# Second attention of a two-layer kernel: query and key rows turned once and stacked through DRAM, output parts summed before a projection over 256 rows

## The chip, the cores and the metric

The kernel runs on one core of one Trainium2 chip. The metric is the device time of one execution in microseconds (us). Three runs of the kernel before gave a median of 1408.72 us, from 1408.67 to 1409.96.

## The reference, cut to what matters

The whole program is two layers over 8 batches of 256 tokens with 256 channels. Each layer norms its input, runs an attention and a feed-forward network on it, and adds attention times silu(feed-forward) to the input. Only the second layer's attention is touched:

```
qkv = einsum('bld,ed->ble', x, w_qkv)            # x: (8, 256, 256)
q, k, v = split into 3 x 16 heads of 16 channels
q = q * rsqrt(mean(q*q) + 1e-6) * q_norm_w       # over the 16 channels
k = k * rsqrt(mean(k*k) + 1e-6) * k_norm_w
scores = einsum('bhqd,bhkd->bhqk', q, k) * 16 ** -0.5
attn = softmax(scores)
out = einsum('bhqk,bhkd->bhqd', attn, v) -> (8, 256, 256)
s = einsum('bld,ed->ble', out, w_proj) + b_proj
g = silu(shared experts + 8 routed experts, top 2)
x = x + s * g
```

Products keep float32 accuracy by splitting each operand into a high part (rounded) and a low part (the rest), and by summing high x high, high x low and low x high: three matmuls for one product (the helper `product`, lines 58 to 60).

## The kernel before, in words

`stage_layer1` is the last of three stages. Its work is laid out in slots, numbered n from -16 to 132; the slots 0 to 127 each carry one head of one batch (n = 16 b + u, head u of batch b). In a slot TensorE runs, in this order: the scores of head n+1 (L1820, two matmuls), the slot's job items, the turn of head n-1's probabilities (L1830, four transposes), and the product of head n-2's probabilities with the values (L1844, four matmuls).

The job items are everything else: T (turn the normed input), Q0 and Q1 (queries and keys), V (values), P0 and P1 (projection of the batch before), L and C (router), g, G, u, U, D0, D1 (the 56 tiles of the feed-forward network, half a product each), and S0 to S7. A planner assigns them to slots: every kind has a cost in units, in which three matmuls of 512 columns are 6 and four transposes 4; the attention's jobs stand at fixed slots; the network's pieces fill each slot up to SLOT_GOAL, less UNIT for the fixed part (30.6 and 10), and from slot -12 to -1 up to EARLY_GOAL (14). Added up over slots 0 to 127 this gives 20.7 units of items per slot, and 202 units before slot 0.

Each engine walks the slots in order and executes its own list for each. VectorE, per slot: the row maximum of head n+1 (L1680), the low part of turned head n-2 (L1684), batch work by u (sum of squares L1602 at u = 2, scaling of the rows L1612 at u = 6, router steps), the first half of the slot's items, the reciprocal of head n+1's sums (L1714), the second half of the items. ScalarE: the high part of the turned head n-2 (L1473), the exponentials of head n+1 (L1465), items. GpSimd: batch work (Newton steps at u = 3, 4, 5, `weigh` L1312 at u = 7, spreading the values), the normalisation of head n+1 (L1337), the network's low parts and masks.

A job writes one of three PSUM banks in turn and waits until the job three before it has given its bank back. There is one bank of scores: the scores of head n wait for the exponentials of head n-1. Turn n-1 and values n-2 in slot n both wait for the low part of head n-2 (L1684).

How queries and keys reach the scores: for every head each row is laid out four times beside itself as high and low parts (`k_hi` L1449 and `q_hi` L1457 on ScalarE, `k_lo` L1619 on VectorE, `q_lo` L1317 on GpSimd). For every pair of heads an S job transposes four 128 x 128 blocks of these (L1773), and ScalarE copies the result out of PSUM to `zq` and `sk` (L1420, L1421), which hold three pairs.

How the output leaves: four heads share one accumulation in PSUM of 128 rows, 16 rows of each head's product with the high part of the values and 16 of that with the low part. It is split as it is (`out_hi` L1479, `out_lo` L1655, at u = 2, 6, 10, 14) and the projection runs over four such groups, 512 rows: 12 matmuls for each P job.

SyncE issues all loads: for each network tile its weights (`load_gu` L1242, `load_d` L1247), masks (`load_cb` L1262), each after a wait for the buffer to come free.

## Time and profile before

| | |
|---|---|
| median of three runs | 1408.72 us |
| the profiled execution itself | 1408.91 us |
| span of its records | 1407.1 us |
| PE (TensorE matmul) busy | 1368.9 us, 97% |
| DVE (VectorE) busy | 920.9 us, 65% |
| ACT (ScalarE) busy | 820.0 us, 58% |
| POOL (GpSimd) busy | 761.9 us, 54% |
| granted TensorE clock, mean | 0.998 |
| DMA engines, mean rate | 118 GB/s |

Busy is the time in which an engine had a recorded instruction running. PE's matmuls overlap at their ends, so what one costs is the distance from its start to the next start, not its length. Idle time of an engine that is not the bound costs nothing.

### The profile page before, as it was taken

Reading aid. Unit: us, or ns where it says so; the run is one execution under the profiler, and the core shown is the slowest. Engines: PE = TensorE matmul, PEld = TensorE weight load, DVE = VectorE, ACT = ScalarE, POOL = GpSimd, SP = SyncE. Lnnn points to the kernel's source line nnn. Section 1 sums busy time; section 2 is a strip of 40 time slices with the busy share of each in tenths; the row PEclk is TensorE's granted clock in tenths of the full one; section 3 lists DMA queues with packets and bytes.
Section 4 is the critical chain, followed back from the end, with each engine's and each line's share of the span. In section 5 each row is a group of like instructions: output and inputs, shape, how many; then the busy total and the mean of one; then the engine's idle time right before and its main releaser. Section 6 shows DMA issues by size and latency. Waiting matters only on the chain. (4 is left out here: it accounts for less than half of the span.)

```text
span 1407.1 us, 25856 instructions
## 1 busy us (share of the span) xinstructions
PE 1368.9 (97%) x8950; PEld 1221.1 (87%) x8950; DVE 920.9 (65%) x1793; ACT 820.0 (58%) x2172; POOL 761.9 (54%) x757
## 2 busy tenths in 40 slices
PE   9999899999999999999999999899999999999997
PEld 7887798999899989998999888788889888889887
DVE  6655566565656565656665665677777878777764
ACT  5553444554544555445544544378787788778873
POOL 2651433454434454435544443477669677777764
PEclk9999999999999999999999999999999999999999
DMA  5995333334332343223433334144233242342442
GB/s 197 323 330 198 85 91 89 92 80 120 100 94 52 101 130 99 75 75 98 114 86 94 113 75 165 68 122 150 83 98 123 68 150 84 120 120 92 143 122 90
DMA packets 85681, 165.64 MB, mean 118 GB/s; under 512 B 16720, under 2 KB 27664, under 8 KB 83248
## 3 DMA queue, kind: packets, MB, share of 16 engines
q1 hardware_dynamic: 85552, 163.99, 38.3%
q8 instruction: 73, 1.20, 0.4%
q14 instruction: 56, 0.46, 0.1%
HBM read 99.90 MB, written 22.09 MB: 87 GB/s over the span
## 5 line engine op out<-in xcount | busy, mean ns | idle before, releaser
L775 POOL TENSOR_TENSOR a_pr<-a_pr,a_ri 128x512 f32<-128x512 f32 x128 | 133.5, 1043 | 299.1 <-DVE a_ri L955 299.1
L832 ACT ACTIVATE a_pr<-a_score,a_nb 128x256 f32<-128x256 f32 x256 | 119.3, 471 | 266.3 <-DVE a_nb L947 266.3
L1337 POOL TENSOR_TENSOR l_pr<-l_pr,l_ri 128x512 f32<-128x512 f32 x128 | 133.5, 1043 | 119.0 <-DVE l_ri L1714 118.1
L1465 ACT ACTIVATE l_pr<-l_score,l_nb 128x256 f32<-128x256 f32 x256 | 119.2, 472 | 80.8 <-DVE l_nb L1680 80.2
L58 PE MATMUL a_job<-s_xs,s_wh 128*128 128x512 f32 x384 | 153.9, 401 | 1.0 <-PEq L221 1.0
L60 PE MATMUL a_job<-s_xs,s_wl 128*128 128x512 f32 x384 | 151.7, 395 | 0.0
L59 PE MATMUL a_job<-s_xs,s_wh 128*128 128x512 f32 x384 | 151.3, 394 | 0.0
L947 DVE TENSOR_REDUCE a_nb<-a_score 128x2 f32<-128x512 f32 x128 | 88.5, 692 | 85.0 <-PE a_score L1026 83.3
L1680 DVE TENSOR_REDUCE l_nb<-l_score 128x2 f32<-128x512 f32 x128 | 87.5, 684 | 34.0 <-PE l_score L1820 33.4
L960 DVE TENSOR_TENSOR a_pt<-a_turn,a_pt 128x512 fp32r<-128x512 f32 x128 | 87.5, 683 | 24.2 <-ACT a_pt L840 24.2
L1844 PE MATMUL l_out<-s_wh,l_vp 128*128 128x256 f32 x512 | 91.6, 300 | 0.9 <-DVE s_wh L1684 0.9
L58 PE MATMUL l_job<-l_xs,s_wl 128*128 128x512 f32 x224 | 90.6, 405 | 1.7 <-DVE l_ga L1594 1.7
L1684 DVE TENSOR_TENSOR s_wh<-l_turn,s_wh 128x512 fp32r<-128x512 f32 x128 | 87.2, 681 | 5.5 <-ACT s_wh L1473 5.4
L1473 ACT ACTIVATE s_wh<-l_turn 128x512 fp32r<-128x512 f32 x128 | 76.5, 597 | 23.4 <-PE l_turn L1830 23.0
L60 PE MATMUL l_job<-l_xs,s_wl 128*128 128x512 f32 x224 | 88.9, 397 | 0.0
L59 PE MATMUL l_job<-l_xs,s_wl 128*128 128x512 f32 x224 | 88.6, 396 | 0.0
L955 DVE RECIPROCAL a_ri<-a_sm 128x2 f32<-128x2 f32 x128 | 21.2, 166 | 102.3 <-ACT a_pr L832 102.3
L1830 PE MATMUL l_turn<-s_ident,l_pr 128*128 128x128 f32 x512 | 77.9, 275 | 10.5 <-DVE s_wh L1684 9.4
L60 PEld LDWEIGHTS a_job<-s_xs,s_wl 128*128 128x128 f32 x384 | 72.1, 188 | 16.9
L1830 PEld LDWEIGHTS l_turn<-s_ident,l_pr 128*128 128x128 f32 x512 | 59.3, 140 | 28.6 <-issue 13.6
L844 ACT ACTIVATE a_ot<-a_out 128x512 fp32r<-128x512 f32 x64 | 38.8, 606 | 77.8 <-PE a_out L60 76.8
L58 PEld LDWEIGHTS a_job<-s_xs,s_wh 128*128 128x128 f32 x384 | 72.2, 188 | 11.3 <-issue 1.4
(257 smaller groups left out, 4780.3 us busy)
## 6 DMA issues: line engine op xcount, KB each, us to landing
s_wl<-wgu_scratch SPq DMA_DIRECT2D x56, 512.0 KB, 4.8
a_sk<-a_rotk SPq DMA_DIRECT2D x384, 64.0 KB, 2.0
a_sq<-a_rotq SPq DMA_DIRECT2D x256, 64.0 KB, 2.0
s_xs<-xn_scratch SPq DMA_DIRECT2D x14, 1024.0 KB, 5.6
l_wd<-wd_scratch SPq DMA_DIRECT2D x56, 256.0 KB, 2.7
a_raw<-in_w SPq DMA_DIRECT2D x30, 256.0 KB, 3.0
wgu_scratch<-f_split SPq DMA_DIRECT2D x14, 512.0 KB, 4.7
f_praw<-in_moe_w SPq DMA_DIRECT2D x14, 384.0 KB, 4.5
```

The costliest lines, as they stand in the source:

```text
L58: pe.matmul(out, lh, rh, start=first, stop=False)
L59: pe.matmul(out, lh, rl, start=False, stop=False)
L60: return pe.matmul(out, ll, rh, start=False, stop=last)
L775: pool.tensor_tensor(e, e, ri[:, n % 2, :].unsqueeze(2).broadcast_to([P, 2, SEQ]), ALU.mult)\
L832: i = act.activation(pr[:, n % 2, t, :], PS[n % 2][:, t * SEQ:(t + 1) * SEQ], ACT.Exp, bias=nb[:, n % 2, t:t + 1], accum_out=sm[:, n % 2, ...
L947: dve.tensor_reduce(nb[:, (n + 1) % 2, :], PS[(n + 1) % 2][:, :].rearrange("p (t k) -> p t k", t=2), AX.X, ALU.max, negate=True).then_inc( ...
L960: dve.tensor_tensor(pt[:, n % 2, 1, :], PT[:, :], pt[:, n % 2, 0, :], ALU.subtract).then_inc(S["turn_free"], 1)
L1337: pool.tensor_tensor(e, e, ri[:, n % 3, :].unsqueeze(2).broadcast_to([P, 2, SEQ]), ALU.mult)\
L1465: i = act.activation(pr[:, n % 3, t, :], PS[n % NPS][:, t * SEQ:(t + 1) * SEQ], ACT.Exp, bias=nb[:, n % 3, t:t + 1], accum_out=sm[:, n % 3 ...
L1680: dve.tensor_reduce(nb[:, (n + 1) % 3, :], PS[(n + 1) % NPS][:, :].rearrange("p (t k) -> p t k", t=2), AX.X, ALU.max, negate=True).then_in ...
L1830: i = pe.transpose(PT[:, kc * SEQ + t * P:kc * SEQ + (t + 1) * P], pr[:, n % 3, t, kc * P:(kc + 1) * P], ident[:, :])
L1844: i = pe.matmul(PO[:, 0:SEQ], vp[:, kc, a, e * P:(e + 1) * P], pt[:, n % 2, q, kc * SEQ:(kc + 1) * SEQ], start=(e == 0 and kc == 0 and q = ...
```

## The change

1. Queries and keys of a head quartet are interleaved by a host-side reordering of the weight's columns (`head_columns`), so that a plain 128-column block of the scaled rows holds eight heads. One job X0 and one X1 for each batch (at u = 8 and 10, for the first batch 8 and 9) transpose these blocks; ScalarE writes the high and VectorE the low part into `tqk`.
2. SyncE stores `tqk` to DRAM (`store_stack`, four DMAs for each X job) and loads it back in stacked form, each high and low row repeated, for four heads at a time (`load_stack`, three DMAs every four slots, first due three slots before the scores that read them). The S jobs, `k_hi`, `q_hi`, `k_lo`, `q_lo` and the copies to `zq` and `sk` are gone.
3. SyncE's list is woven by slots: before each wait of `load_gu`, `load_d` and `store_combine` it issues the stack transfers due up to the slot in which that wait ends (`stack_until`).
4. The high and low product rows of an output group lie 64 rows apart. ScalarE copies 64 rows (`out_low`), VectorE adds the other 64 (`out_sum`), two groups fill 128 rows, and only then are these split (`out_hi` on ScalarE after the exponentials, `out_lo` on VectorE after the reciprocal, every eighth slot, at u = 2 and 10). A P job reads two groups instead of four: 6 matmuls. The first stage splits one piece of projection weights less.
5. The planner's numbers: P costs 6, X costs 4, SLOT_GOAL is 28.1, EARLY_GOAL 18. The same sum over the slots now gives 18.2 units of items per slot for slots 0 to 127, and 250 before slot 0.
6. The sum of squares and the scaling read the rows with a stride of four elements.

```
-    UNIT, SLOT_GOAL, EARLY_GOAL = 10, 30.6, 14
+    UNIT, SLOT_GOAL, EARLY_GOAL = 10, 28.1, 18
...
-        m, r = divmod(n + 4, H1)
-        if r % 2 == 0 and 0 <= m < BATCH:
-            jobs.append((f"S{r // 2}", m))
+        if b + 1 < BATCH and u in X_AT(b + 1):
+            jobs.append((f"X{X_AT(b + 1).index(u)}", b + 1))
...
+                def store_stack(m, half):
+                    wait_free(sp, (f"X{half}", m))
+                    for low in range(2):
+                        sp.dma_start(qs_dram[m % 2, half, :, :, low]..., tqk[:, half, 0, low, :]...)
+                        sp.dma_start(ks_dram[m % 2, half, :, low]..., tqk[:, half, 1, low, :]...)
+                def load_stack(i):
+                    pair = i * PER_LOAD
+                    ...
+                    if p % 4 == 0:
+                        sp.wait_ge(tqk_out[p // 4], 16 * 4 * (m + 1))
+                    if pair >= NSTK:
+                        sp.wait_ge(S["score_full"], 2 * (pair + PER_LOAD - NSTK))
+                    for h in range(2):
+                        sp.dma_start(zq[64 * h:64 * h + 64, h, at, :]..., ...)
+                    sp.dma_start(sk[:, at, :]..., ...)
+                def transfers(n):
+                    m, u = n // H1 + 1, n % H1
+                    if m < BATCH and u - 1 in X_AT(m):
+                        store_stack(m, X_AT(m).index(u - 1))
+                    if n % (2 * PER_LOAD) == 0 and 0 <= n // (2 * PER_LOAD) + 1 < N // (2 * PER_LOAD):
+                        load_stack(n // (2 * PER_LOAD) + 1)
...
+                    elif name[0] == "X":      # ScalarE, then VectorE
+                        act.activation(tqk[:, half, :, 0, :], bank[:, :]..., ACT.Copy)
+                        dve.tensor_tensor(tqk[:, half, :, 1, :], bank[:, :]..., tqk[:, half, :, 0, :], ALU.subtract)
...
-                    for a in range(VG):       # P job
+                    for a in range(VB):
                             i = product(pe, bank[:, 0:D], [ot[:, q, a, ...] ...], [wp[:, q, a, :] ...], ...)
...
+                    if u % (2 * PER_LOAD) == 0:      # scores
+                        pe.wait_ge(zq_in[stack_of(i)], ...)
+                        pe.wait_ge(sk_in[stack_of(i)], ...)
...
-                    own(dve.tensor_reduce(ss[:, :], sqr[:, :, :].rearrange("p t (g d) -> p (t g) d", d=D1), AX.X, ALU.add))
+                    own(dve.tensor_reduce(ss[:, :]..., sqr[:, :, :].rearrange("p t (g d q) -> p (t g) q d", d=D1, q=4), AX.X, ALU.add))
```

## Rows read from the trace of the kernel before

**Rows 1.** Windows of stage three: busy us of each engine, clock, DMA.

```profile
889.90:918.70 28.80, 25.95 (x134) 20.86 (x135) 20.32 (x50) 13.48 (x30) 17.46 (x25) 0.94 0.27 92
918.70:1383.90 465.20, 451.61 (x3153) 406.40 (x3152) 351.68 (x746) 360.57 (x1057) 342.14 (x419) 1.00 0.38 115
```

**Rows 2.** Tile view of the scores: count, min/median/max ns, first and last start.

```profile
L1820 PE MATMUL l_score<-l_sk,l_zq x256: 275/280/386, 918.7 to 1383.9; 128*128 128x256 f32 x128
```

**Rows 3.** Waits between 920 and 1385 us: total, times, longest.

```profile
PE l_turn L1830 <- DVE s_wh L1684: 9.4, 14, 1.3
```

**Rows 4.** Timeline of PE: start us, length us; slots 50 to 52.

```profile
1105.37 0.41 PE L1820 MATMUL l_score<-l_sk,l_zq 128*128 128x256 f32 x2
1105.61 0.38 PE L1773 MATMUL l_job<-s_ident,l_stq 128*128 128x128 f32 x2
...
1105.96 0.48 PE L58 MATMUL l_job<-l_xs,s_wl 128*128 128x512 f32 x1
...
1107.43 0.60 PE L1830 MATMUL l_turn<-s_ident,l_pr 128*128 128x128 f32 x4
1107.79 0.72 PE L1844 MATMUL l_out<-s_wh,l_vp 128*128 128x256 f32 x4
1108.35 0.40 PE L1820 MATMUL l_score<-l_sk,l_zq 128*128 128x256 f32 x2
...
1112.85 0.28 PE L58 MATMUL l_job<-s_wl,l_ot 128*128 128x256 f32 x1
...
1114.27 0.38 PE L1773 MATMUL l_job<-s_ident,l_stq 128*128 128x128 f32 x2
```

**Rows 5.** Groups by line and shape, 900 to 1400 us: busy, mean ns, idle before.

```profile
L1465 ACT ACTIVATE l_pr<-l_score,l_nb 128x256 f32<-128x256 f32 x256 | 119.2, 472 | 80.8 <-DVE l_nb L1680 80.2
...
L1684 DVE TENSOR_TENSOR s_wh<-l_turn,s_wh 128x512 fp32r<-128x512 f32 x128 | 87.2, 681 | 5.5 <-ACT s_wh L1473 5.4
...
L1420 ACT ACTIVATE l_zq<-l_job 64x256 fp32r<-64x256 f32 x128 | 48.0, 375 | 1.5 <-PE l_job L1773 0.5
...
L1619 DVE TENSOR_TENSOR l_stk<-l_qk,l_stk 128x256 fp32r<-128x256 f32 x32 | 23.1, 762 | 0.0
```

**Rows 6.** Timeline of PE, the start of slot 34 (batch 2, u = 2).

```profile
1047.71 0.39 PE L1820 MATMUL l_score<-l_sk,l_zq 128*128 128x256 f32 x2
```

**Rows 7.** Timeline of DVE in slot 34.

```profile
1049.35 0.41 DVE L1655 TENSOR_TENSOR l_ot<-l_out,l_ot 128x256 fp32r<-128x256 f32 x1
1049.68 1.21 DVE L1602 TENSOR_REDUCE l_ss<-l_sqr 128x64 f32<-128x1024 f32 x1
...
1051.26 0.16 DVE L1714 RECIPROCAL l_ri<-l_sm 128x2 f32<-128x2 f32 x1
1051.34 0.67 DVE L1598 TENSOR_TENSOR l_ga<-l_ga,l_job 128x512 f32<-128x512 f32 x1
```

**Rows 8.** Timeline of POOL, the weighing of batch 3's queries.

```profile
1067.91 1.30 POOL L1312 TENSOR_TENSOR l_qk<-l_qk,s_nqk 128x512 f32<-128x512 f32 x1
```

**Rows 9.** Timeline of PE, the start of slot 40 (batch 2, u = 8).

```profile
1069.00 0.28 PE L1820 MATMUL l_score<-l_sk,l_zq 128*128 128x256 f32 x1
```

**Rows 10.** Tile view of wgu_scratch: SyncE's issue, ns; then issue to landing.

```profile
L1242 SPq DMA_DIRECT2D s_wl<-wgu_scratch x54: 319/427/586, 890.3 to 1373.2; - x54
...
DMA to landing us min/median/max: 3.3/4.7/10.7
```

**Rows 11.** Page, part 6: DMA issues of stage two, KB each, us to landing.

```profile
a_sk<-a_rotk SPq DMA_DIRECT2D x384, 64.0 KB, 2.0
```

**Rows 12.** Timeline at the head and the tail of stage three.

```profile
909.40 0.51 PE L58 MATMUL l_job<-l_xs,s_wl 128*128 128x512 f32 x1 [1.67 <-DVE l_ga L1594]
...
1398.36 0.42 DVE L1655 TENSOR_TENSOR l_ot<-l_out,l_ot 128x256 fp32r<-128x256 f32 x1 [1.25 <-ACT l_ot L1479]
1398.70 1.28 DVE L1668 SCALAR_TENSOR_TENSOR l_y<-l_yt,l_y 128x512 f32<-128x512 f32 x2
...
1399.57 0.28 PE L58 MATMUL l_job<-s_wl,l_ot 128*128 128x256 f32 x1
```

More of the change, by code:

```diff
@@ L40 @@
 TB = SEQ // P
-VG, VSTRIDE, VBLK = 4, 160, 640
+VG, VB, VSTRIDE, VBLK = 4, 2, 144, 576
+VHALF = VG * D1
 ROOT_BITS = float(0x5F3759DF - (1 << 22))
@@ L1196, in stage_layer1 @@
         gu_in = l1.gu_in
+        zq_in, sk_in = ([n_.sem(f"{s}_in{i}") for i in range(NSTK // PER_LOAD)] for s in ("zq", "sk"))
+        tqk_out = [n_.sem(f"tqk_out{i}") for i in range(2)]
         d_in, cb_in = ([n_.sem(f"{s}_in{i}") for i in range(3)] for s in ("d", "cb"))
@@ L1200, in stage_layer1 @@
             "own", "consts", "zeroed", "vp_zeroed", "job_full", "xs_hi", "v_hi", "spread",
-            "sq_ready", "ms_ready", "newton", "scaled", "weighted", "k_hi", "q_hi", "k_lo", "q_lo",
+            "sq_ready", "ms_ready", "newton", "scaled", "weighted", "turned_hi",
             "score_full", "max_ready", "exp_ready", "sum_inv", "norm_ready", "turn_full", "turn_hi", "turn_free",
-            "pv_done", "out_hi", "out_free", "tanh_ready", "gate_done", "cmul", "hid_hi", "hid_lo", "down_done",
+            "pv_done", "out_low", "out_free", "out_hi", "out_lo", "tanh_ready", "gate_done", "cmul", "hid_hi", "hid_lo", "down_done",
             "lg_exp", "cm_ready", "y_ready", "y_tanh", "y_act", "gated", "merged", "last_merged", "stored")}
@@ L1223, in tokens @@
             return slice(at, at + P)
-        def heads(t, part, half):
-            at = part * D + half * P
-            return qk[:, t, at:at + P].rearrange("p (h d) -> p h d", d=D1).unsqueeze(2).broadcast_to([P, 8, 2, D1])
-        def half_of(rows, t, half):
-            return rows[:, t, 8 * half:8 * half + 8]
         def wait_merged(engine, s):
@@ L1313, in weigh @@
                         .then_inc(S["weighted"], 1)
-                def q_lo(m, half, t):
-                    pool.wait_ge(S["q_hi"], 4 * m + 2 * half + t + 1)
-                    pool.tensor_tensor(half_of(stq, t, half)[:, :, 1::2, :].bitcast(F32R), heads(t, 0, half),
-                                       half_of(stq, t, half)[:, :, 0::2, :], ALU.subtract).then_inc(S["q_lo"], 1)
                 def spread(m, a):
@@ L1558, in job_out @@
                         if m >= 1 and t == 0:
-                            dve.wait_ge(S["q_lo"], 4 * m)
-                            dve.wait_ge(S["k_lo"], 4 * m)
+                            wait_full(dve, ("X1", m - 1))
                         dve.tensor_copy(qk[:, t, :], bank[:, :]).then_inc(free_of(item), 1)
+                    elif name[0] == "X":
+                        half = int(name[1])
+                        dve.wait_ge(S["turned_hi"], 2 * m + half + 1)
+                        dve.tensor_tensor(tqk[:, half, :, 1, :], bank[:, :].rearrange("p (r n) -> p r n", r=2),
+                                          tqk[:, half, :, 0, :], ALU.subtract).then_inc(free_of(item), 1)
                     elif name[0] == "P":
@@ L1714, in _ @@
                         dve.reciprocal(ri[:, (n + 1) % 3, :], sm[:, (n + 1) % 3, :]).then_inc(S["sum_inv"], 1)
+                    if n >= 10 and (n - 10) % 8 == 0 and (n - 10) // 8 < VB * BATCH:
+                        out_lo((n - 10) // 8)
                     for item in second:
@@ L1896, in tile_weights, with head_columns @@
     return np.stack(tiles)
+def head_columns(w):
+    import numpy as np
+    qk = w[0:2 * D].reshape(2, 2, 4, 2, D1, D).transpose(0, 1, 3, 4, 2, 5).reshape(2 * D, D)
+    return np.concatenate([qk, w[2 * D:]])
 def proj_rows(w):
     import numpy as np
-    rows = [[(VG * a + p // (2 * D1)) * D1 + p % D1 for p in range(P)] for a in range(VG)]
+    rows = [[(2 * VG * j + p // D1) * D1 + p % D1 for p in range(P)] for j in range(VB)]
     return np.concatenate([w[r] for r in rows], axis=1)
```

167 lines of the change are left out of this document (88 added, 79 removed).

## The prediction

> **What bounds the kernel now.** I read the windows first. From the first score matmul to the last (918.7 to 1383.9) TensorE is busy 451.6 of 465.2 us, 97%; VectorE follows with 351.7 (76%), ScalarE 360.6 (78%) and GpSimd 342.1 (74%), at a full clock and with the DMA engines busy 38% of the time [rows 1]. The reader is to see one engine full and three with a fifth or more to spare. The tile view of the scores gives the pace: 127 slots in 465.1 us, 3.66 us each [rows 2]. Then the waits: the largest that TensorE's matmuls have is the turn's wait for VectorE's low part, 9.4 us in 14 places, none longer than 1.3 us [rows 3]. So stage three is TensorE's issue stream with short hiccups, and the timeline of PE prices that stream by start-to-start distances [rows 4]:
> - scores 1105.61 - 1105.37 = 0.24, turn 1107.79 - 1107.43 = 0.36, values 1108.35 - 1107.79 = 0.56: 1.15 us fixed per slot (unrounded starts of many slots give the same);
> - an S job, 1105.96 - 1105.61 = 0.35;
> - a P job, twelve matmuls, 1114.27 - 1112.85 = 1.42, so 0.118 each; a network half product (6 units) is three matmuls at twice that, 0.70. One planner unit is thus 0.1175 us.
>
> Check: 1.15 + 20.7 units x 0.1175 = 3.58 us, against 3.66 measured. The difference, 0.08 x 127 = 10 us, is stalls, a little more in truth since the S jobs cost 3 units and are planned at 4. The stalls that I can place lie in slots with extra VectorE work: router steps, row scaling at u = 6, `k_lo` at u = 8 and 12.
>
> **The change part by part.** TensorE's own work first.
> 1. S jobs: 64 x 0.355 = 22.7 us go; 16 X jobs of the same four transposes come, 16 x 0.355 = 5.7. Net -17.0.
> 2. Projection: 16 P jobs lose 6 of 12 matmuls, 96 x 0.118 = 11.3. Net -11.3.
> 3. EARLY_GOAL moves 48 units (5.6 us) of network work ahead of slot 0; it is moved, not saved: the first score comes later and the slots are shorter.
> Sum: **-28.3 us**. The new regular slot is 1.15 + 18.2 x 0.1175 = 3.28 us. These are all on the path, because TensorE is the path.
>
> What the change gives back or takes elsewhere:
> 4. *Relief.* `k_lo` takes 23.1 us off VectorE, where its pieces averaged 762 ns; the X jobs' low parts bring 16 x 0.681 = 10.9 [rows 5], one in each of two slots of a batch. On ScalarE the copies to `zq` alone were 48.0 us [rows 5], and `sk`, `k_hi` and `q_hi` go as well, against 16 copies of 512 columns; GpSimd loses `q_lo`. By the distances of the score starts, about half of the 10 us of stalls lies in the slots of `k_lo` and the next two. I take -4 (from 0 to -8).
> 5. *`out_lo` is later, and P0 waits for it.* It used to stand before the sum of squares; now it stands after the reciprocal. In slot 34, which starts at 1047.71 [rows 6], `out_lo` ended at +2.05 us and the reciprocal began at +3.55, behind the sum of squares [rows 7]. The new `out_lo` follows there: +3.55 + 0.08 + 0.41 = +4.1, or +4.7 where the first half of the items holds a G or U (about 0.6, the distance from 1051.34 to its end [rows 7]). The next slot starts at +3.28, so it is ready at +0.8 or +1.4 of slot u = 3, and P0 stands at 0.24 (b = 6, 7), 0.6 (b = 1, 4) or 1.3 us (b = 2, 3, 5) by the planned items. The seven waits: 0.8, 0.1, 0.1, 0.2, 0.1, 0.6, 1.2, with a semaphore's 0.1 each: 4 us. They take the place of about 1.3 us of turn stalls in the same slots. +2.7 (0 to +6). Behind P0 on TensorE stand the whole rest of the slot and the next scores.
> 6. *X0 waits for the weighed queries.* S0 came at u = 12; X0 comes at u = 8, right behind the scores in four batches. In batch 2's turn GpSimd ended `weigh` at 1067.91 + 1.30 = 1069.21 [rows 8], 0.2 us into slot 40 [rows 9]. With the two slots before it 0.4 us shorter each, that is 1.0 us into it, and X0 wants it at 0.24. Over seven batches (some have a G or U ahead of X0, and in those with router steps VectorE holds these slots long anyway) I take 4 us, of which 1.5 replaces old stalls. +2.5 (0 to +7).
> 7. *Tightness.* The slack of turn and low part shrinks with the slot: `out_lo`, right behind maximum and low part, began at +1.64 us [rows 6, 7], so these end about 1.75 us after the slot's start, and the turn wanted them 0.9 us before its end, at 2.7 before and at 2.4 now. VectorE goes from 76% to about 341/430 = 79%. +2 (0 to +10).
> 8. *Stack through DRAM, steady state.* 31 later loads, each three issues at 0.43 us [rows 10], due three slots (9.8 us) before they are read. The nearest landings are 2.0 us for 64 KB [rows 11] and 4.7 us, at worst 10.7, for 512 KB [rows 10]; with 1.3 us of issues that is 3.3 to 6.0, at worst 12.0. I take the middle: hidden, 0. SyncE issues about 160 more DMAs, 69 us of its queue in 430, where it spends most of the time waiting; what is queued behind a stack wait there is the network's next weights, which have four slots.
> 9. *Stack, first batch.* X0 of batch 0 needs the bank of U0, which came free only when TensorE went on at 909.40 [rows 12]; then its split (about 2 us with VectorE's queue), X1's, eight stores at 0.43, the router's store and mask load ahead of it in SyncE's list, three loads and a landing of 2.0 to 4.7: about 922 to 925. TensorE, with 48 units more, reaches the first score at 918.7 + 5.6 = 924.3. So 0 to 1 us late; I take +1 (0 to +4).
> 10. *Tail.* Part of the -28.3 is 1.4 us for the last two P jobs. But between the last values and P0 there are now four steps instead of two (two more like the 0.42 of [rows 12]), and the last `out_lo` stands behind the two final activations of 1.28 us [rows 12]: 1398.36 + 0.42 + 1.28 + 0.45 = 1400.5 against P0 at 1399.57 before [rows 12]. 1.4 saved, 1.2 lost on the path: +1.2.
> 11. The strided sum of squares and scaling, the smaller memset, the one piece less in stage one (where ScalarE and GpSimd work beside TensorE): 0 each, from -1 to +1 for stage one. For the stride no row of the trace has its like; between nothing and one more pass of 1.21 us [rows 7] I take the nearest row, its own, unchanged.
>
> A page speaks against this. The Trainium skill's "SBUF — State Buffer", section on the DMA port swizzle, says that SBUF has 16-byte lines and that accesses which each cross to a new line pay a penalty; the new reduce steps 16 bytes between elements. No run here shows it yet. By that rule the sum would be that of rival B below, not mine.
>
> Sum: -28.3 - 4 + 2.7 + 2.5 + 2 + 0 + 1 + 1.2 = -22.9. From the profiled execution's own 1408.91 us this is **1386.0 us**. That execution lies 0.2 us above the median of the three runs, less than any term.
>
> **The rivals.**
> A. *All of it arrives.* The relief removes the old stalls and no new ones come: -28.3 - 4 + 1.2 = -31, 1378 us. For it: slot 50, planned at 16 units, took 1108.35 - 1105.37 = 2.98 us [rows 4], what its matmuls cost and nothing more, and three engines are freed. Against: items 5 and 6, where the code puts the new consumer one slot behind its producer.
> B. *Strided VectorE work costs double.* The sum of squares takes 2.4 instead of 1.21 us in slot u = 2, right ahead of `out_lo`, and the scaling in u = 6 grows likewise ahead of `weigh`. Both are ahead of a TensorE wait already short of time: 7 x (0.9 + 0.7) = 11 us, 1397 us. For it, only what is said above; the one strided pass of the trace leaves it open: `k_lo` averages 762 ns for 256 columns [rows 5] beside 0.41 for `out_lo`'s plain pass of that size [rows 7], but its undisturbed pieces were as short as the plain one.
> C. *The chain through the engines becomes the bound.* The loop of one head is maximum 0.68, two exponentials 0.94 [rows 5], reciprocal 0.16 and a second-half item 0.67 [rows 7], and some 0.3 for semaphores and reading the sums: 2.8 us against 3.28. Should crowded slots hold it at 0.1 us over in the mean, that is 127 x 0.1 = 13 us: 1399 us. For it: VectorE at 79% in strict order. Against: the loop has 0.5 us to spare, and the ends of slots absorb.
> D. *Slower: the stacks come late.* TensorE waits at each fourth slot for `zq` and `sk`. The gain is 22.9 / 31 = 0.74 us per load, so it decides once a landing takes more than 9.8 - 1.3 + 0.74 = 9.2 us; at 10.7, the worst landing of rows 10, each wait is 2.2 us and the time 1386 + 68 = 1454, at 9.6 it is 1.1 us and 1420. For it: the loads pass in one queue with 512 KB weights and stores of the same rows. Against: the median landing is half of that, and the DMA engines have 60% to spare.
>
> **How the numbers follow.** Chances: forecast (1380 to 1393) 0.60, A 0.14, B 0.08, C 0.12, D 0.06. Two runs of this kernel differ by less than 0.2%, about 3 us, so that is the bound of "same". Everything but D is faster by more than 10 us; I leave 0.02 for a mixture that ends within 3 us of before. Faster 0.93, same 0.02, slower 0.05. The range takes in A below and most of C above: 1376 to 1400.
>
> **What would show it.** In the changed profile: L1773's successor with 64 instead of 256 transposes, and 96 fewer matmuls on `l_ot`; scores 3.3 to 3.4 us apart; the first score at 924 to 926 us; waits of TensorE for `out_lo` (seven, about 4 us) and for `weigh` (up to seven, about 4 us); landings of the stack loads of 3 to 6 us with no wait of the scores behind them; L1602's successor at 1.2 us. The prediction is wrong if the scores wait for a DMA, if the reduce goes to 2 us or more, or if the slots stay above 3.45 us with TensorE busy under 95%.

## The result and the profile after

The changed kernel took 1505.64 us (median of four runs, 1505.45 to 1510.36) beside 1409.34 us for the kernel before on the same chip: ratio 1.0688, 95% interval 1.0663 to 1.0713. The forecast was 1386.0. Rival D, the late stacks, happened; the time lies 52 us above the higher of the two that it named (1420 and 1454), so D was not all of it.

The page of the changed kernel (profiled execution 1510.36 us): busy time of each engine, granted clock in 40 slices, and the chain that ended last.

```profile
span 1508.6 us, 25052 instructions
...
PE 1368.9 (91%) x8662; PEld 1212.5 (80%) x8662; DVE 919.1 (61%) x1793; ACT 757.9 (50%) x1947; POOL 741.4 (49%) x724
...
PEclk9999999999999999999999998989999989989899
...
DMA l_sk<-ks_scratch 7%; PE l_job L59 2%; PE l_job L61 2%; PE l_job L60 2%; POOL l_pr L1374 2%; DVE l_nb L1704 2%; PE l_turn L1855 1%; PE l_out L1869 1%; DVE s_wh L1708 1%; PE l_score L1845 1%; PE l_down L1766 1%; SPq L1283 1%; PE l_down L1768 1%; PE l_down L1767 1%; POOL l_ga L1381 1%
```

A chain that was TensorE's now has a DMA of the change at its head. Windows of stage three, ahead of the first score and from first to last, answer to [rows 1]; the tile view answers to [rows 2].

```profile
889.90:944.90 55.00, 33.09 (x166) 26.98 (x167) 23.85 (x54) 11.77 (x21) 17.67 (x24) 0.81 0.42 126
944.90:1484.60 539.70, 446.24 (x2846) 393.31 (x2847) 345.50 (x739) 299.22 (x840) 322.88 (x387) 0.92 0.44 138
```

```profile
L1845 PE MATMUL l_score<-l_sk,l_zq x256: 275/280/553, 944.9 to 1484.6; 128*128 128x256 f32 x128
```

The stages ahead end within 1 us of where they did before, so all is lost here: the first score is 26.2 us later (944.9 for 918.7; I had +6.6) and the 127 slots take 539.7 us for 465.1, 74.6 more instead of some 29 fewer. TensorE is busy 83% of that stretch, the three others at most 64%; no engine is the bound. The clock of 0.92 says that TensorE ran part of this time at its lower level.

The waits of the changed kernel's TensorE, and of GpSimd, from 890 to 1500 us (total, times, longest), answer to [rows 3]:

```profile
PE l_score L1845 <- DMA l_sk<-ks_scratch: 76.5, 13, 18.9
PE l_turn L1855 <- DVE s_wh L1708: 18.4, 24, 3.9
PE l_job L59 <- DVE l_ot L1679: 6.7, 6, 2.0
PE l_down L1766 <- DVE l_y L1686: 5.2, 2, 3.6
```

```profile
POOL l_ga L1381 <- DMA l_cb<-ct_scratch: 56.9, 11, 13.6
```

The first line is the result: 18.9 us ahead of the first score, 57.6 us behind it, of which 47.9 in six waits for the first stack of a batch, the one that is loaded right behind the batch's stores. The last, GpSimd's, shows that it is not the stack's own matter: the mask load, which the change does not touch, now makes GpSimd wait as well (with both transfers split, below, 15.1 us). The tile view of `sk` has the issue lengths of its loads in ns (min/median/max) and the time from issue to landing in us; the timeline of SyncE shows long issues beside usual ones (start us, length us; x2 is two issues):

```profile
L1286 SPq DMA_DIRECT2D l_sk<-ks_scratch x32: 539/566/6888, 931.5 to 1460.6; - x32
...
DMA to landing us min/median/max: 8.1/10.0/16.3
```

```profile
913.04 0.56 SPq L1269 DMA_DIRECT2D qs_scratch<-l_tqk  x1
...
917.42 2.52 SPq L1269 DMA_DIRECT2D qs_scratch<-l_tqk  x1
...
923.42 0.34 SPq L1254 DMA_DIRECT2D ct_scratch<-l_ct  x1
929.46 0.35 SPq L1263 DMA_DIRECT2D l_cb<-ct_scratch  x1
...
930.32 1.11 SPq L1283 DMA_DIRECT2D l_zq<-qs_scratch  x2
...
937.10 5.09 SPq L1283 DMA_DIRECT2D l_zq<-qs_scratch  x2
942.23 3.87 SPq L1286 DMA_DIRECT2D l_sk<-ks_scratch  x1
```

The median landing, 10.0 us, is near what I had put as the worst, 10.7. And some issues themselves take 2.5 to 6.9 us, and every load queued behind them waits too. What holds them the trace does not say; in the kernel before none took over 1.5 us in this stage, in e3, with both transfers split, none over 2.02. In this stretch the mask load stood at 923.8 for its store, which was behind the eight stack stores; so the first stack load left at 930.3.

What a late stack does to TensorE afterwards: windows ahead of, in, and behind one such wait, then the same matmul form at either clock (timeline of PE).

```profile
995.00:1001.90 6.90, 6.30 (x43) 5.34 (x41) 4.81 (x13) 4.53 (x13) 3.97 (x4) 1.00 0.64 190
1001.90:1011.20 9.30, 0.14 (x2) 0.02 (x1) 0.61 (x2) 1.12 (x2) 4.61 (x6) 0.74 0.51 165
1011.20:1016.20 5.00, 4.99 (x17) 4.31 (x18) 2.04 (x4) 1.03 (x4) 2.07 (x2) 0.50 0.17 58
```

```profile
1000.50 0.39 PE L60 MATMUL l_job<-l_xs,s_wl 128*128 128x512 f32 x1
1000.73 0.39 PE L61 MATMUL l_job<-l_xs,s_wl 128*128 128x512 f32 x1
...
1011.21 0.76 PE L1845 MATMUL l_score<-l_sk,l_zq 128*128 128x256 f32 x2 [9.17 <-DMA l_sk<-ks_scratch]
...
1012.20 0.63 PE L60 MATMUL l_job<-l_xs,s_wl 128*128 128x512 f32 x1
1012.63 0.63 PE L61 MATMUL l_job<-l_xs,s_wl 128*128 128x512 f32 x1
```

A step of 0.23 us before the wait is 0.43 after it: while TensorE idled for 9.2 us the grant fell from 2.4 to 1.2 GHz, and the matmuls that follow pay double until it is back. By the clocks of the two windows of stage three above, (1 - 0.81) x 2 x 55.0 + (1 - 0.92) x 2 x 539.7 = 21 + 86 us were at the lower level; the clock's own record has 82 for the second. Where TensorE works, half of such a stretch is lost; where it waits, nothing.

### The profile page after: what moved, and what is told of

The parts are those of the page before. It is cut to its first block and busy times, and to the rows that moved or that the text cites. A ratio compares the mean times of both kernels' runs of the same rounds, so it can differ in the third digit from the quotient of the medians.

```text
span 1508.6 us, 25052 instructions
## 1 busy us (share of the span) xinstructions
PE 1368.9 (91%) x8662; PEld 1212.5 (80%) x8662; DVE 919.1 (61%) x1793; ACT 757.9 (50%) x1947; POOL 741.4 (49%) x724
## 5 line engine op out<-in xcount | busy, mean ns | idle before, releaser
L832 ACT ACTIVATE a_pr<-a_score,a_nb 128x256 f32<-128x256 f32 x256 | 119.6, 472 | 266.5 <-DVE a_nb L947 266.5
L1481 ACT ACTIVATE l_pr<-l_score,l_nb 128x256 f32<-128x256 f32 x256 | 119.6, 472 | 179.9 <-DVE l_nb L1704 179.8
L1845 PE MATMUL l_score<-l_sk,l_zq 128*128 128x256 f32 x256 | 54.1, 294 | 77.7 <-DMA l_sk<-ks_scratch 76.5
L1845 PEld LDWEIGHTS l_score<-l_sk,l_zq 128*128 128x128 f32 x256 | 40.6, 196 | 80.7 <-issue 78.9
L1855 PE MATMUL l_turn<-s_ident,l_pr 128*128 128x128 f32 x512 | 81.3, 283 | 19.3 <-DVE s_wh L1708 18.4
L59 PE MATMUL l_job<-l_xs,s_wl 128*128 128x512 f32 x224 | 94.8, 423 | 0.0
L60 PE MATMUL l_job<-l_xs,s_wl 128*128 128x512 f32 x224 | 93.7, 418 | 0.0
L61 PE MATMUL l_job<-l_xs,s_wl 128*128 128x512 f32 x224 | 93.6, 418 | 0.0
L1381 POOL TENSOR_TENSOR l_ga<-l_ga,l_cb 128x512 f32<-128x512 f32 x44 | 56.5, 1285 | 57.0 <-DMA l_cb<-ct_scratch 56.9
```

What stands on the lines that cost most here:

```text
L59: pe.matmul(out, lh, rh, start=first, stop=False)
L60: pe.matmul(out, lh, rl, start=False, stop=False)
L61: return pe.matmul(out, ll, rh, start=False, stop=last)
L832: i = act.activation(pr[:, n % 2, t, :], PS[n % 2][:, t * SEQ:(t + 1) * SEQ], ACT.Exp, bias=nb[:, n % 2, t:t + 1], accum_out=sm[:, n % 2, ...
L1481: i = act.activation(pr[:, n % 3, t, :], PS[n % NPS][:, t * SEQ:(t + 1) * SEQ], ACT.Exp, bias=nb[:, n % 3, t:t + 1], accum_out=sm[:, n % 3 ...
L1845: i = pe.matmul(PS[n % NPS][:, t * SEQ:(t + 1) * SEQ], zq[:, u % 2, r, t * P:(t + 1) * P], sk[:, r, :], start=True, stop=True)
```

## The experiments

All times are medians; each ratio is to the kernel before on the same chip. "Slots" is the time from first to last score. The kernel before took 1409.42 us beside e1, e2, e3 and o1, 1408.95 beside f1, f2, f3 and h1, 1409.56 beside g1, g2, s1 and h2, 1409.37 beside k1 and o2, 1409.76 beside o3 and o4.

### The shape of the transfers: e1, e2, e3

The load of `zq` had the zero-stride repeat (2) as its source's outermost dimension, the store of `ks` the head parity (2). e1 splits the first by its repeat, e2 the second by its parity, e3 both: the same bytes to the same places, by more DMAs.

```
e1: - sp.dma_start(zq[64 * h:64 * h + 64, h, at, :]..., own.unsqueeze(0).broadcast_to([2, 2 * D1, PER_LOAD * SEQ]))
    + for rep in range(2):
    +     lo = 64 * h + 32 * rep
    +     sp.dma_start(zq[lo:lo + 32, h, at, :]..., own)
e2: - sp.dma_start(ks_dram[m % 2, half, :, low].rearrange("h d p n -> h (d p) n"), tqk[:, half, 1, low, :]...)
    + for h in range(2):
    +     sp.dma_start(ks_dram[m % 2, half, h, low]..., tqk[64 * h:64 * h + 64, half, 1, low, :]...)
```

> Changed kernel; each stack load of zq is issued as four DMAs of 32 rows instead of two whose source repeats 32 rows by an outermost dimension of two. Same bytes, same places. Theory 1 (a DMA is spread over as many of the 16 DMA engines as its outermost dimensions allow, so the zq loads and the ks stores, both with an outermost two, run on two engines and everything behind them queues): the zq loads are two thirds of the bytes on those two engines, so the sk loads land in 5 us or less in mid-batch, the scores' wait of 76.5 us falls below 40, time 1425 us (1405 to 1450). Theory 2 (the way through DRAM takes long by itself, or SyncE is late by its order): 64 more DMAs in SyncE's queue, 1505 us or more. Theory 3 (bytes through the 64 partitions of a half are the limit): bytes and partitions are the same, 1505 us.

> Changed kernel; each store of the key rows is issued as two DMAs of 64 rows instead of one whose outermost dimension is two. The zq loads stay as they are. Theory 1: a third of the bytes leave the two engines, and those just ahead of the first stack of a batch, where the scores waited longest; time 1475 us (1450 to 1495), the waits at the batch boundaries (slot 14, 54 us in sum) down by a third. Theories 2 and 3: 1505 us or a little more.

> Changed kernel with both splits. Theory 1: no transfer is left on two engines; sk landings 3 to 5 us, the scores wait for DMA under 10 us in sum, first score near 926 us instead of 945, time 1395 us (1385 to 1408): the forecast's 1386 plus the strided sum of squares (2.0 instead of 1.2 us, 7 times ahead of a wait of TensorE). Theory 2: 1505 us or more, since SyncE issues 96 more DMAs. Theory 3: 1505 us.

Measured: e1 1457.8 us, 1.0341 [1.0316, 1.0366]; e2 1473.75, 1.0453 [1.0437, 1.0469]; e3 1426.14, 1.0117 [1.0100, 1.0134]. So -48, -32 and together -79.5 us. The two rivals of e1 to e3 (the way through DRAM or SyncE's order; the bytes through half of the partitions) wanted 1505 or more and are out. The shape as the cause had 1405 to 1450 for e1, a miss by 8 us, 1450 to 1495 for e2, met, and 1385 to 1408 for e3, a miss by 18: it is right and not the whole loss. e3's waits of TensorE, its landing of `sk`, and its window from first to last score:

```profile
PE l_turn L1857 <- DVE s_wh L1710: 16.9, 22, 2.9
PE l_job L59 <- DVE l_ot L1681: 11.0, 7, 2.0
PE l_score L1847 <- DMA l_sk<-ks_scratch: 10.8, 4, 6.6
...
PE l_job L1799 <- POOL l_qk L1356: 4.8, 5, 1.7
```

```profile
DMA to landing us min/median/max: 3.0/4.8/8.0
```

```profile
931.60:1400.60 469.00, 426.50 (x2846) 378.10 (x2847) 343.49 (x739) 297.49 (x840) 322.87 (x387) 0.98 0.56 162
```

The `sk` load itself is untouched in e3, yet it lands in 4.8 us for 10.0: it had stood behind the others. Not the bytes and not the number of issues are the cost, for the first were the same and the second higher, but the shape of the two DMAs. In the window the DMA engines move 162 GB/s instead of 138 and the clock is 0.98 instead of 0.92.

The Trainium skill's "DMA: Bandwidth & Descriptors", section "Why a DMA increments its semaphore by 16 and not by 1", has the rule: the number of engines of a DMA is the largest up to 16 that divides the slowest dimension above one on both sides, and on a hardware queue they are always the lowest-numbered; its checklist names a leading zero-stride repeat as the case to avoid. By it both DMAs had two engines, the same two. e1 to e3 agree in sign and in both places. The trace's record of semaphores says more: on the two semaphores of the `zq` loads it has 192 updates by DMA for 64 loads, 3 each, and on those of the stores 608 for 32 of `qs` and 32 of `ks`, which is 16 and 3; every load of `sk` and of the weights has 16. In e3 each part of `zq` and `ks` has 16 too. That agrees with few engines for just these two; how many, and which, is not recorded.

### What the stride costs: f1

f1 is e3 with ScalarE writing the squares in the order in which VectorE's sum reads them, so that the reduce steps by one element.

```
- act.activation(sqr[:, int(name[1]), :], bank[:, :], ACT.Square)
+ act.activation(sqr[...].rearrange("p (g q d) -> p g d q", d=D1, q=4), bank[...].rearrange("p (g d q) -> p g d q", d=D1, q=4), ACT.Square)
- dve.tensor_reduce(ss[...], sqr[...].rearrange("p t (g d q) -> p (t g) q d", d=D1, q=4), AX.X, ALU.add)
+ dve.tensor_reduce(ss[:, :], sqr[...].rearrange("p t (g d) -> p (t g) d", d=D1), AX.X, ALU.add)
```

> Both splits, and ScalarE writes the squares in the order in which VectorE reduces them, so that the sum of squares reads elements side by side again (ScalarE's write has the stride now). If the stride is what made the reduce 2.0 instead of 1.2 us: 1.2 us again, TensorE's wait for out_lo (11 us in seven places) down by about 0.8 each, time 1426 - 5.5 = 1420 (1416 to 1424). If VectorE's time there is hidden: 1426, within 2.

1421.78 us, 1.0095 [1.0078, 1.0113]: 4.4 us less by the medians, 3.1 by the ratios, whose intervals just overlap. Groups by form from 890 us on (total us, mean ns): two lines of the changed kernel, then two of f1.

```profile
L1624 DVE TENSOR_REDUCE l_ss<-l_sqr 128x64 f32<-128x1024 f32 x8 | 16.0, 2002 | 0.2
L1447 ACT ACTIVATE l_sqr<-l_job 128x512 f32<-128x512 f32 x16 | 9.6, 600 | 3.3 <-PE l_job L61 3.3
```

```profile
L1626 DVE TENSOR_REDUCE l_ss<-l_sqr 128x64 f32<-128x1024 f32 x8 | 9.7, 1217 | 0.2
L1449 ACT ACTIVATE l_sqr<-l_job 128x512 f32<-128x512 f32 x16 | 17.2, 1073 | 2.8 <-PE l_job L61 2.8
```

The reduce's step of four elements adds 0.79 us to its 1.21 on VectorE; the write that replaces it has a step of sixteen and adds 0.47 to 0.60 us on ScalarE. Off VectorE it is cheaper for the kernel, because TensorE waits there for `out_lo` (11.0 us in e3, 7.5 in f1). The scaling is no second case, though item 6 of the change calls it strided: its view has the four interleaved heads innermost, so it goes through the rows element by element, and takes 1239 ns here and 1240 in g1, whose columns are plain.

### Moving the consumers: f2, f3

f2 is f1 with P0 and P1 at u = 4 and 5 (not for the last batch), f3 is f2 with X0 and X1 of the later batches at u = 9 and 11.

```
f2: - if u in (3, 4) and b >= 1:           jobs.append((f"P{u - 3}", b - 1))
    + first = 3 if b == BATCH else 4
    + if u in (first, first + 1) and b >= 1: jobs.append((f"P{u - first}", b - 1))
f3: - return (8, 9) if m == 0 else (8, 10)
    + return (8, 9) if m == 0 else (9, 11)
```

> As f1, and the jobs P0 and P1 of all batches but the last stand one slot later, at u = 4 and 5, so that out_lo is done before them. If TensorE's waits at u = 3 are the wait for out_lo: the loss of slot u = 3 (15 us summed over the batches in the run with both splits) falls under 5, time 1412 (1407 to 1417) if f1 gives 1420. If VectorE's backlog behind the sum of squares holds TensorE anyway, by the low part of the next head, the loss moves to the turn in the same slots: no more than 3 us under f1.

> As f2, and X0 and X1 of all batches but the first stand at u = 9 and 11 instead of 8 and 10. If TensorE waits at u = 8 for the weighed queries: the loss of slots 7 and 8 (13 us) halves, time 5 us under f2. Against it, the first stack of a batch is loaded a slot later behind its stores: if the scores wait for it, up to 7 x 2 us come back. I expect f2 minus 2 (minus 6 to plus 6).

f2 1423.81 us, 1.0113 [1.0097, 1.0128]; f3 1426.38, 1.0125 [1.0110, 1.0140]. f2 misses its 1412, f3 its 2 us under f2; neither is faster than f1. The removed wait came back one place on. f2's waits:

```profile
PE l_turn L1858 <- DVE s_wh L1711: 23.3, 32, 1.6
...
PE l_job L59 <- DVE l_ot L1682: 1.9, 1, 1.9
```

The six waits for `out_lo` at u = 3 are gone (5.6 us in f1; the 1.9 us left belong to the tail), and the turn waits 6.8 us more than in f1 (16.5). That fits a VectorE late in these slots, so that whatever TensorE asks of it first pays.

### Plain columns, more early work, the stack alone: g1, g2, s1, k1

g1 leaves the columns in their old order, so nothing is strided; the stores then go by 32 rows, eight for each X job, and the `zq` load is four DMAs. g2 is g1 with SLOT_GOAL 27.8 and EARLY_GOAL 21. s1 is g1 without the output part (P of 12 matmuls, SLOT_GOAL 28.85). k1 is f1 with g2's two numbers.

```
g1: - head_columns(i["L1_attn_w_qkv"]).T
    + i["L1_attn_w_qkv"].T
    + for p in range(4):                       # in store_stack
    +     rows = tqk[32 * p:32 * p + 32, half]
    +     sp.dma_start(qs_dram[...][..., p], rows[:, 0])
    +     sp.dma_start(ks_dram[...][..., p], rows[:, 1])
g2, k1: - UNIT, SLOT_GOAL, EARLY_GOAL = 10, 28.1, 18
        + UNIT, SLOT_GOAL, EARLY_GOAL = 10, 27.8, 21
```

> Whole change, but the weight columns keep their order (heads one after the other), so that neither the squares, nor the sum of squares, nor the scaling has a stride; the rows go to DRAM in eight stores per X job, each spread over 16 engines, and come back in four loads of zq and one of sk as in e3. Nothing left out. Against f1 (1421.8) it takes the strided write off ScalarE (1.07 to 0.6 us, 14 times) and adds 32 DMA issues: 1418 us (1414 to 1423); sum of squares 1.2 us, squares 0.6 us.

> g1 with EARLY_GOAL 21 instead of 18 and SLOT_GOAL 27.8 instead of 28.1: 36 more units (4.2 us) of network work before slot 0, where TensorE waits for the first stack (8 us, and 10 us at half clock). If that wait is simply filled: 4 to 6 us under g1. If the added network pieces hold up VectorE and SyncE ahead of the first stack, the first score moves back by as much: g1.

> g1 without the output part: the output is split and projected over four groups of 512 rows as before, SLOT_GOAL 28.85. By the prediction's booking it must be 10 us slower than g1, which has that much less work on TensorE. By tightness (o1_output_only won nothing, h1 4 of 11 us) it is within 3 us of g1, 1415 to 1421.

> The changed kernel with both split transfers and the squares written in the reduce's order, and the planner's goals moved to 27.8 per slot and 21 ahead of slot 0 (the first score then some 4 us later, about 936, and the slots 0.04 us shorter in plan). Theory 'the first stack is late' (8 us of wait and a half-clock stretch at 931 us are lost there): the added early work covers the wait; 1410 to 1416, wait of the scores under 4 us. Rival 'tightness takes it back' (shorter slots lose what the covered wait gains): 1419 to 1425, with more wait of turn and projection for VectorE than the 25 us of before.

g1 1434.15 us, 1.0160 [1.0134, 1.0185]; g2 1427.31, 1.0127 [1.0111, 1.0143]; s1 1429.31, 1.0141 [1.0123, 1.0159]; k1 1421.96, 1.0086 [1.0071, 1.0101]. g1 was put at 1418, below f1; it has plain passes everywhere and is 12 us slower. SyncE issued its 16 first stores back to back from 913.7 to 924.0 us, and the first score came at 935.5, 3.8 us later than in f1. The rest lies in the slots, where the scores wait 9.0 us for later stacks for f1's 2.4 and the clock was down for 20.8 us for f1's 8.0. g2 nearly ended the scores' wait and gained 6.8 us by the medians (the intervals overlap). k1 shows where that ends. Its waits:

```profile
PE l_turn L1857 <- DVE s_wh L1710: 21.8, 29, 2.3
PE l_job L59 <- DVE l_ot L1681: 8.2, 6, 1.9
...
PE l_job L59 <- DMA s_wl<-wgu_scratch: 5.6, 1, 5.6
...
PE l_score L1847 <- DMA l_sk<-ks_scratch: 1.8, 2, 0.9
```

The scores' wait went from 10.6 to 1.8 us, but the early work now waits for its own weights, which stand behind the stores in SyncE's list (5.6 us), and the turn gave back another 5.3: no gain over f1, as the rival said. s1 is 4.8 us faster than g1 by the medians, with intervals that overlap, where the prediction's sum wants it 10 us slower; so in the whole change the output part did not pay for itself, although it takes 11.3 us of matmuls away.

### The output part and the pure removal: o1 to o4, h1, h2

o1 is the kernel before with edit 4 alone. o2 is o1 with P0 and P1 one slot later (f2's edit). h1 is the kernel before whose P jobs read two of the four groups, so half of the projection is left out, and nothing takes its place. h2 is h1 which also leaves out the low part of the keys for seven of eight heads. o3 and o4 are o1 and o2 with `out_lo` behind the second half of the items.

```
o1: + out_low, out_sum, out_hi, out_lo, P over VB = 2 groups, as in edit 4; SLOT_GOAL 29.85
h1: - for a in range(VG):      SLOT_GOAL 30.6, P_ = 12
    + for a in range(2):       SLOT_GOAL 29.85, P_ = 6
h2: + k_lo on [:, 0:1, 2:4, :] only, the low part of `stk` set to zero once
o3, o4: - if n >= 10 and (n - 10) % 8 == 0 and ...: out_lo((n - 10) // 8)
          for item in second: job_out(item)
        + if n >= 10 and (n - 10) % 8 == 0 and ...: out_lo((n - 10) // 8)
```

> Kernel before with the output part of the change alone (two parts summed, projection over 256 rows, one projection piece less in stage one, SLOT_GOAL 29.85, the six units per P job spread over the slots); queries and keys as before, no stacks in DRAM, no strided reduce. By the sum of the prediction: -11.3 of matmuls, +1.2 at the tail, +2 to +3 for out_lo behind the sum of squares: 1401.5 us (1397 to 1405). If the later out_lo costs what the matmuls bring: 1409.

> Kernel before, with only the first two of the four output groups read by each projection job (6 instead of 12 matmuls; the other two groups are left out of the result), P costed at 6 and SLOT_GOAL 29.85. Nothing is added anywhere, so it is the pure value of 11.3 us less of TensorE's work, which the prediction booked in full. If TensorE alone is the bound: 1409.4 - 11.3 = 1398. If the other engines' chain takes over as the slots shrink (the prediction's term of 2 us for tightness too small): 1404 to 1409; o1_output_only, with the same matmuls saved and 1409.2 us, then owes its missing gain to tightness and not to the later out_lo.

> h1, and VectorE splits only one of eight key heads into its low part (the others' low parts are left out, zero instead): some 18 us less of VectorE's work, nothing else. If VectorE's load is what stopped h1 from gaining its 11.3 us: 1400 us (1398 to 1402), the 11 us nearly whole. If the stalls come from elsewhere (ScalarE, GpSimd, order): 1404, as h1.

> The kernel before with the output part alone (two parts summed, projection over two groups of 256 rows in all, SLOT_GOAL 29.85), and P0 and P1 of all batches but the last at u = 4 and 5 instead of 3 and 4. Theory 'P0 waits for the late low part': the projection alone with less work gained 4.3 us, the whole output part gained nothing; with P a slot later the wait for the low part is gone and the time is about 1405. Rival 'the added VectorE work holds the turn instead': 1408 to 1411, with the turn's wait for VectorE above 14 us.

> o1 (the kernel before with the output part alone) with out_lo behind the second half of VectorE's items instead of right behind the reciprocal. In o1 eight of sixteen out_lo passes took 0.9 to 1.27 us, each where a GpSimd pass had begun just before; the others 0.41. Both of its inputs are now in SBUF, while the kernel before read one from PSUM and took 0.41 every time. Theory 'GpSimd's pass holds VectorE's': the normalisation that the reciprocal releases is over or nearly so when out_lo comes; mean below 0.6 us for 0.72, the turn's wait for VectorE from 14.3 to about 11 us as in the pure removal, 1405 to 1408 us less what P0 then waits (1 to 3 us). Rival 'the position does not matter, the slots are full': mean stays near 0.7, 1409 to 1412.

> o2 (o1 with P0 and P1 at u = 4 and 5) with the same move of out_lo. P has a slot more to wait in, so the move costs nothing there. Theory 'GpSimd's pass holds VectorE's': below o3 by P0's wait, 1405 to 1407. Rival 'P at u = 4 and 5 is itself the bad place' (o2 was 5.8 us above o1): 1412 to 1416, as o2.

| | us | ratio | turn waits for VectorE | P waits for `out_lo` |
|---|---|---|---|---|
| o1 | 1409.23 | 0.9999 [0.9990, 1.0009] | 14.3 | 1.7 |
| h1 | 1404.65 | 0.9972 [0.9960, 0.9985] | 11.0 | |
| h2 | 1402.85 | 0.9952 [0.9937, 0.9968] | 10.3 | |
| o2 | 1415.03 | 1.0039 [1.0026, 1.0051] | 17.0 | |
| o3 | 1419.06 | 1.0059 [1.0038, 1.0081] | 14.9 | 9.2 |
| o4 | 1417.38 | 1.0052 [1.0032, 1.0072] | 20.0 | |

h1 is the cleanest number of the study: 11.3 us of matmuls gone, no work added, 4.3 us gained. Where the rest went its window from first to last score says, beside the second line of [rows 1]; behind it, one of its waits and the stretch that follows:

```profile
918.80:1381.70 462.90, 444.93 (x3061) 399.64 (x3060) 349.87 (x744) 358.77 (x1057) 341.52 (x417) 0.99 0.37 116
```

```profile
1035.67 0.36 PE L1742 MATMUL l_down<-l_wd,l_hid 128*128 128x256 f32 x1 [1.81 <-POOL l_hid L1348]
```

```profile
1036.60:1040.00 3.40, 3.40 (x13) 2.71 (x12) 1.22 (x3) 0.74 (x3) 1.15 (x2) 0.50 0.00 0
```

TensorE idles 18.0 us (462.9 - 444.9) for 13.6 before, 4.4 more. And its busy time fell by 6.7 us only: twice, here and at 1234.6, its clock was at 1.2 GHz for 3.4 us, fully busy, which the profile of before has nowhere between its scores. That costs up to 3.4 us. The runs say the same: the mean clock was 0.992 to 0.998 in h1's ten, 0.998 to 1.0 in the thirteen of before beside them. So of the 7.0 us that did not arrive 4.4 are waits, and the rest can be clock.

h2 gains 1.8 us more by the medians; the intervals overlap. Its cut leaves one eighth of `k_lo`'s columns, and still took only 7.7 of its 23.6 us away. o1, which has h1's matmuls, is 4.6 us above it (3.8 by the ratios); the work it adds is 16 passes net on VectorE and 16 on ScalarE, engines with a quarter and a fifth of their time free.

o2 to o4 all miss, and on the same side. o3 shows what a wait of P0 costs: `out_lo` moved behind the items made P0 wait 9.2 us for 1.7, and the kernel is 9.8 us slower than o1; most of the rest is clock, for o3's slots have 10.2 us at the lower level and o1's 3.4. In o4, with P a slot later, no wait of P for `out_lo` is left, and the turn pays instead (20.0 for 14.3). o2 is 5.8 us over o1, of which its profile, 1411.79 us and the shortest of its six, shows 1.3. The clock again can hold much of the rest: 0.994 to 0.997 in o2's runs, 0.9955 in the mean, 0.9982 in o1's. The difference is an estimated 2 x 0.0027 x 1415 = 7.6 us at half speed, worth up to 3.8.

One thing lies behind both `k_lo` and `out_lo`. First the tile view of h2 and that of o1 (count, min/median/max ns); then o1's timelines of VectorE and of GpSimd at two `out_lo`.

```profile
L1619 DVE TENSOR_TENSOR l_stk<-l_qk,l_stk x32: 177/232/1592, 909.2 to 1318.1; 128x32 fp32r<-128x32 f32 x32
```

```profile
L1671 DVE TENSOR_TENSOR l_ot<-l_os,l_ot x16: 402/416/1269, 958.6 to 1400.7; 128x256 fp32r<-128x256 f32 x16
```

```profile
988.95 0.41 DVE L1671 TENSOR_TENSOR l_ot<-l_os,l_ot 128x256 fp32r<-128x256 f32 x1
...
1017.70 1.26 DVE L1671 TENSOR_TENSOR l_ot<-l_os,l_ot 128x256 fp32r<-128x256 f32 x1 [0.28 <-ACT l_ot L1485]
```

```profile
989.11 1.14 POOL L1338 TENSOR_TENSOR l_pr<-l_pr,l_ri 128x512 f32<-128x512 f32 x1 [2.52 <-DVE l_ri L1730]
...
1017.64 1.04 POOL L1338 TENSOR_TENSOR l_pr<-l_pr,l_ri 128x512 f32<-128x512 f32 x1
```

At 988.95 VectorE began first: its pass took 0.41 us and GpSimd's 1.14. At 1017.64 GpSimd began first, by 0.06 us, took its usual 1.04, and VectorE's pass ended only 0.28 us after it, at 1.26. The same with 32 columns in `k_lo`: 0.18 us alone, up to 1.59. Seven of the sixteen `out_lo` of o1 are long, 0.90 to 1.27 us; the others take 0.40 to 0.43. In the kernel before, `out_lo` read one operand from PSUM and took 0.407 to 0.425 us in all 32 cases; the output part made both operands SBUF. The Trainium skill's "SBUF — State Buffer", section "SBUF: two separate sides", states it: a VectorE operation with two SBUF inputs and a GpSimd operation that reads SBUF hold a shared port pair in turn, each for its whole instruction. The rows agree. In o1 this comes to 16 x (0.72 - 0.41) = 5 us of VectorE's time, close to the 4.6 (3.8) us over h1. That the one is the other's cause was not shown: o3 and o4 only brought the mean from 0.72 to 0.66 us, since behind the items other GpSimd passes are under way. In the whole change it plays a small part (e3: median 0.403 us, longest 1.484).

## Why the prediction was wrong, by its steps

**Step 8 failed, in the way that rival D describes.** "I take the middle: hidden, 0" rested on landings of DMAs of another shape: the 64 KB and 512 KB of the nearest rows [rows 10, 11]. Size was matched, shape was not. In its place: 10.0 us median for `sk`, 76.5 us of waits of the scores (18.9 of them before the first), and clock lost behind the long ones. e3 gives 79.5 of the 119.6 us by which the forecast was off back with the same bytes. D's threshold, a landing of 9.2 us, was crossed by the median, and its price for all later loads, 34 to 68 us, holds the 57.6 measured; but they did not come at each fourth slot, 47.9 us of them came at six batch starts, and D had neither the late first score nor the clock. Its chance of 0.06 was too low, for "the DMA engines have 60% to spare" is a mean over 16 engines and says nothing of a DMA that uses few of them. The mean share in the changed slots is 0.44, still under half.

**Step 9** had the first score at 924.3 + 1. With mended shapes it is 931.6 (e3). X0 and its split came on time (first store at 912.1 in e3), but a store issue took about 0.6 us, not 0.43, the mask load waited for its store in the same list, and the scores waited 6.6 us. k1 shows that one cannot simply lay more work over it.

**Step 11** failed as rival B said: the reduce took 2.00 us for 1.21. It cost less than B's 11 us: 3 to 4 us from e3 to f1, with the stride moved to ScalarE. "The nearest row, its own, unchanged" was a choice against a written rule, with no row for it; the end of the range, one more pass of 1.21 us, was the better guide. The other half of B, a scaling that grows likewise, could not come: the scaling has no stride (1239 ns, 1240 with plain columns).

**Step 5** had 4 us in seven waits for `out_lo` at u = 3. Six came, of batches 1 to 6, 9.1 us in e3 and 5.6 in f1: the place was right; 3.5 us of the miss is the slower reduce ahead of it, the rest is open. o3 agrees with the premise that behind P0 everything on TensorE stands (9.8 us slower for 7.5 us more of this wait, part of the rest being clock). **Step 10**, the tail, had 0.2 us less; it got 0.8 longer (last score to the end: 23.18 us before, 23.94 in f1), with a wait of 1.9 us for the last `out_lo`.

**Step 6** was right: up to seven waits for `weigh`, 4 us in sum; e3 has five, 4.8 us in sum.

**Steps 1 and 2 were right as counts and wrong as gains; step 7, tightness, was the term undersized:** +2, at most 10. With the transfers and the reduce mended, in f1, what is left shows in its window from first to last score, beside 451.61 us busy of 465.20 in [rows 1]; one wait that the prediction had nowhere stands behind it.

```profile
931.70:1393.60 461.90, 424.80 (x2847) 374.85 (x2848) 338.54 (x739) 302.36 (x840) 323.05 (x387) 0.99 0.56 165
```

```profile
PE l_down L1768 <- DVE l_y L1688: 5.2, 2, 3.6
```

By steps 1 to 7 these slots should have taken 465.2 - 26.9 (steps 1 and 2 without the last two P jobs) - 5.6 (step 3) + 3.2 (steps 4 to 7) = 435.9 us; they took 461.9, 26.0 more. TensorE's idle time in them went from 13.6 to 37.1 us, 23.5 more where 3.2 had been put. It is all in named waits: the turn +7.1 (9.4 to 16.5), `out_lo` 5.6, X0 4.9, the network's second product for VectorE's `l_y` +4.0 (1.2 to 5.2), the stacks after the first 2.4, together 24.0. Only the turn's is step 7's own. The other 5.7 us are TensorE's own time that did not fall as booked; f1 has 8.0 us at the lower clock there and the kernel before none, up to 4.0 us of it.

h1 measures tightness alone: of 11.3 us removed 7.0 did not arrive, though VectorE, ScalarE and GpSimd had over a fifth of their time free and got no new work. My reading, which fits and is not shown, is that their lists, laid out by slot and in order, were already as late as TensorE in the slots with batch work, so that a shorter slot exposes them. f2, f3, o2 and o4 speak against a single badly placed consumer: in each the moved wait came back at the turn. h2, with 7.7 us less on VectorE, gained 1.8, so VectorE's load is a part at most. The trace of f1 says why the low part cannot be all of it. All 26 waits of the turn end with it, but in ten GpSimd's normalisation, for which the turn waits as well, ended within the same wait, seven times 0.06 us earlier:

```profile
1019.16 1.04 POOL L1376 TENSOR_TENSOR l_pr<-l_pr,l_ri 128x512 f32<-128x512 f32 x1 [1.35 <-DVE l_ri L1738]
1019.58 0.68 DVE L1710 TENSOR_TENSOR s_wh<-l_turn,s_wh 128x512 fp32r<-128x512 f32 x1
1020.41 0.63 PE L1857 MATMUL l_turn<-s_ident,l_pr 128*128 128x128 f32 x4 [0.65 <-DVE s_wh L1710]
```

An earlier low part alone would give back an estimated 9.0 of the 16.5 us, the sum of the distances to the later of GpSimd's end and the wait's start. Step 4, the relief, was not measured by itself: taking `k_lo` down by 7.7 us in h2 gained 1.8, while the whole 23.1 had been given 4 beside the tightness that it was to offset.

**The other rivals.** C, "the chain becomes the bound", put 13 us and names the mechanism nearest to what is left in f1; but its loop of 2.8 us fits in the 3.28 of a regular slot, and by the step prices the loss sits in slots u = 1 to 3, 7, 8, 11, 13 and 14, not in all. That GpSimd's pass of the same loop ends so close to the turn's start in ten waits speaks for C in those slots. A (all arrives) is excluded by h1.

**The sum, from f1 to the forecast:** its profiled execution, 1419.4 us, lies 33.4 above 1386.0: 6.4 in the first score (931.7 for 925.3), 26.0 in the slots, 1.0 in the tail; the median of f1 is 2.4 higher still. Which engine's order in which slot makes the turn late was not settled, nor why the clock falls more often when the slots are shorter. No version that does the whole computation was measured faster than the kernel before; o1 is equal to it.

## What to carry to other kernels

Take a DMA's price only from a row of the same shape: compare the outermost dimension of both sides, not the bytes, and put a large one outermost (or split by the small one) before anything else is tuned; one narrow DMA delays what stands behind it in the queue, and a long wait that it makes costs TensorE its clock as well. Matmul time taken out of a pipeline that is 97% full was gained in part only, here 4 of 11 us: read the slack slot by slot, not from busy shares, and compare the clock of two profiles before a difference of a few us is given to a wait. Before moving a consumer, ask whether the producer's engine is late as such; if so, the wait moves with it.
